# Group norm, 4-bit quantise and grouped 1x1 convolution: unrolled pipeline, ring of 12 images, coefficients for two images at a time

## The chip, the cores and the metric

The kernel runs on one core of a Trainium2 chip. The metric is device time in microseconds (us) of one execution, from the first to the last instruction and what the launch puts around them. It was measured three times before the change.

The core has five engines that run side by side, each in its own program order, and wait for one another on semaphores: TensorE (PE in the rows; PEld is its weight load), VectorE (DVE), ScalarE (ACT), GpSimd (POOL) and SyncE (SP), which here only issues DMAs.

## The reference, cut to what matters

`x` is (32, 512, 28, 28) in float32: 32 images, 512 channels, 784 pixels. Everything is one layer:

```python
v = _gn(x)                       # group norm: 32 groups of 16 channels, over 16*784 values, eps 1e-5
xg = v.reshape(B, 4, 128, H, W)[:, [1, 2, 3, 0]]
xa = round(clip((xg - lA) / (uA - lA), 0, 1) * 15) / 15
wq = (round(clip((weight - lW) / (uW - lW), 0, 1) * 15) / 15 - 0.5) * 2
y  = einsum('bgihw,goi->bgohw', xa, wq.reshape(4, 128, 128))
inv = gamma / sqrt(running_var + 1e-5)
y  = relu(y * inv + (beta - running_mean * inv))
out = x + (y + v)
```

## The kernel before, in words

**Tiling.** An image is `[128 partitions, 4 groups, 784]` float32, 1568 KB. Channel group g is a 128-channel slab, the contraction of one matmul. `images` is a ring of 8 such slots (`RING`). SP loads images in order, stores image n when DVE has added its four groups (semaphore `final`), and after each store issues the load that goes into the slot of the image before (L185 to L191). Most loops are hardware loops of 8 images with the first two and last six peeled off (`over_images`, L146).

**Per image, per engine, in program order:**

- DVE (`image` in the vector block): `cap` of groups 0 and 1 (min with 15, int16 to bf16, L409), statistics of the image two ahead (`bn_stats`, L398, six halves of 392 pixels: groups 0 to 2), `cap` of groups 2 and 3, a reciprocal of the standard deviation (L404), then `finish` for four groups (L420): `images = max(prod, floor) + images`, one operand from PSUM.
- ACT: the affine `images*y_scale + y_bias` of group 3 (L262); sum and squares of group 3 of the image two ahead (L223, L232); then `quantise` of the next image: four activations that write `levels` as int16 (L254), with `copy_mean` (L238) between the second and third, and `deviation` (L243, L244) behind them.
- POOL: `coefficients` of this image (L342 to L352, ten small instructions, a Newton step on `rough`), `sum_subsets` of the next (L321, L323), one `affine` of the image before (L360), `deviations` of the next (L330 to L335), which waits for `copy_mean`, and two `affine`s of this image.
- PE: `average_deviations` (L498) of the next image, four `multiply` of six matmuls each (L518: three bf16 parts of the weights times two halves), then `average_stats` (L492, L494).

Small instructions in one engine that read each other's result are fenced by a semaphore (`linked`, `chained`). The matmuls with `avg` sum over the 16 channels of a norm group. `prod` in PSUM has three sets of two banks; `PSUM_SET` gives set 0 to groups 0 and 3.

So the order of an image's coefficients is: statistics (DVE, ACT), sums (POOL), means (PE), copy (ACT), deviations (POOL), variance (PE), copy and root (ACT), reciprocal (DVE), coefficients (POOL), quantise (ACT), cap (DVE), matmuls (PE), and, with the affine of POOL, the addition (DVE).

Of the kernel before, what the change touches and what calls it, by code (L numbers as in the profile page):

```python
# [6 lines left out]
ACT = mybir.ActivationFunctionType  # L7
F32 = mybir.dt.float32
# [10 lines left out]
RING = 8  # L19
HEAD = 2  # L20
PARTS = 3
Y_ON_POOL = 3
STATS_ON_DVE = 3
PSUM_SET = (0, 1, 2, 0)
AHEAD = 2
# [3 lines left out]
def fused_norm_quantised_conv(nc, x, weight, limits, channel_params, out):  # L29
# [6 lines left out]
    SUBSETS = 4  # L36
    COUNT = HW // SUBSETS
    PAIRS = PER_NORM * SUBSETS
    assert C == G * P and B % RING == 0 and HALF <= nc.vector.BN_STATS_FMAX and HALF % 2 == 0

    TRIPS = B // RING
    x_v = x.rearrange("(t j) (g p) h w -> t j p g (h w)", p=P, j=RING)
    out_v = out.rearrange("(t j) (g p) h w -> t j p g (h w)", p=P, j=RING)

    with ExitStack() as ctx:
# [9 lines left out]

# [5 lines left out]
        stats = sb("stats", [P, 2, G, SUBSETS, 3], F32)  # L61
        x_sum = sb("x_sum", [P, 1], F32)
        unused = sb("unused", [P, HW], BF16)
        pair_sums = sb("pair_sums", [P, G, 2, 3], F32)
        stat_sums = sb("stat_sums", [P, 2, G, 3], F32)
        gmean = sb("gmean", [P, 2, G], F32)
        dev = sb("dev", [P, G, SUBSETS], F32)
        dev2 = sb("dev2", [P, G, SUBSETS], F32)
        dev2_pairs = sb("dev2_pairs", [P, G, 2], F32)
        dev2_sum = sb("dev2_sum", [P, G], F32)  # L70
        std = sb("std", [P, 2, G], F32)
        half_var = sb("half_var", [P, 2, G], F32)
        rough = sb("rough", [P, 2, G], F32)
        newt = sb("newt", [P, 3, G], F32)
        three_halves = sb("three_halves", [P, G], F32)
        rstd = sb("rstd", [P, G], F32)
        mean_q = sb("mean_q", [P, G], F32)
        mean_rstd = sb("mean_rstd", [P, G], F32)
        q_scale = sb("q_scale", [P, 2, G], F32)
        q_bias = sb("q_bias", [P, 2, G], F32)  # L80
        y_scale = sb("y_scale", [P, 2, G], F32)
        y_bias = sb("y_bias", [P, 2, G], F32)

# [8 lines left out]
        w_rng = sb("w_rng", [P, 3], F32)  # L92
        a_rng = sb("a_rng", [P, 4], F32)
        bn = sb("bn", [P, 8, G], F32)
        bias_bn = sb("bias_bn", [P, G], F32)
        floor = sb("floor", [P, G], F32)
        eps = sb("eps", [P, 3], F32)
        early = sb("early", [P, 1], F32)
        ident = sb("ident", [P, P], F32)
        avg = sb("avg", [P, P], F32)  # L100
        avg_n = sb("avg_n", [P, P], F32)

        prod = ps("prod", [P, 3, 2, 512], F32)
# [10 lines left out]
        weights_in = sem("weights_in")  # L114
        consts_done = sem("consts_done")
        eps_done = sem("eps_done")
        cols_done = sem("cols_done")
        bn_var_in = sem("bn_var_in")
        bn_std_done = sem("bn_std_done")
# [3 lines left out]
        params_ready = sem("params_ready")  # L123
        prep_step = sem("prep_step")
        consts_step = sem("consts_step")
        stats_done = sem("stats_done")
        moments_step = sem("moments_step")
        stats_summed = sem("stats_summed")
        mean_summed = sem("mean_summed")
        mean_ready = sem("mean_ready")  # L130
        dev_ready = sem("dev_ready")
        var_summed = sem("var_summed")
        std_ready = sem("std_ready")
        rough_ready = sem("rough_ready")
        coef_ready = sem("coef_ready")
        coef_step = sem("coef_step")
        quantised = sem("quantised")
        capped = sem("capped")
        y_ready = sem("y_ready")
        y_rest = sem("y_rest")  # L140
        multiplied = sem("multiplied")
        final = sem("final")

        def over_images(engine, image):  # L146


            for j in range(HEAD):
                image(0, j)  # L150
            with engine.Fori(0, TRIPS - 1) as t:
                for j in range(HEAD, HEAD + RING):
                    image(*later(t, 0, j))
            for j in range(HEAD, RING):
                image(TRIPS - 1, j)

        def output_group(g):

            return (g + G - 1) % G

        def later(t, j, by):
            return t + (j + by) // RING, (j + by) % RING

        def inside(t, j, by=0):

            return not isinstance(t, int) or 0 <= RING * t + j + by < B

        block = ctx.enter_context(nc.Block())

        @block.sync  # L170
        def _(sync):
            for g in (0, G - 1, 1, 2):
                sync.dma_start(images[:, 0, g], x_v[0, 0][:, g]).then_inc(first_loaded[g], DMA)
            sync.dma_start(w_raw[:], weight.rearrange("(g o) i -> o g i", o=P)).then_inc(weights_in, DMA)

            def load(t, j):
                if inside(t, j, -RING):
                    sync.wait_ge(stored[j], DMA * t)
                sync.dma_start(images[:, j], x_v[t, j]).then_inc(x_loaded[j], DMA)

            def store(t, j):
                sync.wait_ge(final, G * (RING * t + j) + G)
                sync.dma_start(out_v[t, j], images[:, j]).then_inc(stored[j], DMA)

            for j in range(1, RING):  # L185
                load(0, j)
            store(0, 0)
            with sync.Fori(0, TRIPS - 1) as t:
                for j in range(1, 1 + RING):
                    store(*later(t, 0, j))  # L190
                    load(*later(t, 0, j + RING - 1))  # L191
            for j in range(1, RING - 1):
                store(TRIPS - 1, j)
            for g in range(G):
                o = output_group(g)
                sync.wait_ge(final, G * (B - 1) + g + 1)
                sync.dma_start(out_v[TRIPS - 1, RING - 1][:, o],
                               images[:, RING - 1, o]).then_inc(stored[RING - 1], DMA)
            for j in range(RING):
                sync.wait_ge(stored[j], DMA * (TRIPS + (G - 1 if j == RING - 1 else 0)))  # L200

        @block.scalar
        def _(act):
            act.dma_start(rows[:], channel_params.rearrange("k (g p) -> (k g) p", p=P)).then_inc(rows_in, DMA)
            act.dma_start(bounds[:], limits.to_broadcast([P, 4])).then_inc(limits_in, DMA)
            act.wait_ge(eps_done, 1)

            nc.scalar.activation(early[:], eps[:, 0:1], ACT.Sqrt, bias=eps[:, 1:2])
            act.wait_ge(cols_done, 1)
            nc.scalar.activation(cols[:], cols_ps[:, 0:4 * G], ACT.Identity).then_inc(bn_var_in, 1)  # L210
            act.wait_ge(bn_var_in, 1)
            nc.scalar.activation(bn[:, 0], cols[:, 3], ACT.Sqrt, bias=eps[:, 1:2]).then_inc(bn_std_done, 1)

            last = G - 1

            def take_sum(t, j):

                n = RING * t + j
                if isinstance(t, int) and n == 0:
                    act.wait_ge(first_loaded[last], DMA)  # L220
                else:
                    act.wait_ge(x_loaded[j], DMA * t + (DMA if j else 0))
                nc.scalar.activation(unused[:], images[:, j, last], ACT.Identity,  # L223
                                     accum_out=x_sum[:]).then_inc(moments_step, 1)
                act.wait_ge(moments_step, 3 * n + 1)
                nc.scalar.activation(stats[:, j % 2, last, :, 1], x_sum[:].to_broadcast([P, SUBSETS]), ACT.Identity,
                                     scale=1.0 / HW).then_inc(moments_step, 1)

            def take_squares(t, j):

                act.wait_ge(moments_step, 3 * (RING * t + j) + 2)
                nc.scalar.activation(unused[:], images[:, j, last], ACT.Square, scale=-1.0,  # L232
                                     bias=stats[:, j % 2, last, 0, 1:2],
                                     accum_out=stats[:, j % 2, last, 0, 2:3]).then_inc(moments_step, 1)

            def copy_mean(t, j):
                act.wait_ge(mean_summed, RING * t + j + 1)
                nc.scalar.activation(gmean[:, j % 2], mean_ps[:, 0:G], ACT.Identity).then_inc(mean_ready, 1)  # L238

            def deviation(t, j):  # L240
                par = j % 2
                act.wait_ge(var_summed, RING * t + j + 1)
                nc.scalar.activation(half_var[:, par], var_ps[:, 0:G], ACT.Identity, bias=eps[:, 2:3], scale=0.5)  # L243
                nc.scalar.activation(std[:, par], var_ps[:, 0:G], ACT.Sqrt, bias=eps[:, 0:1]).then_inc(std_ready, 1)  # L244

            def quantise(t, j):
                n, par = RING * t + j, j % 2
                act.wait_ge(coef_ready, n + 1)
                if inside(t, j, -2):
                    act.wait_ge(capped, 2 * (n - 2) + 2)  # L250
                for g in range(G):
# [4 lines left out]
                if inside(t, j, 1):  # L256
                    deviation(*later(t, j, 1))
# [302 lines left out]
```

## Time and profile before

| what | us |
|---|---|
| runs of the kernel before | 298.91 (median), 296.23, 301.08 |
| span of the profiled execution, first to last instruction | 293.8 |
| median less this span | 5.1 |
| span over 32 images | 9.2 |
| DMA: 103.18 MB, mean 351 GB/s over the span | |

The profiled execution's own time is not given beside its span. The median of the runs less the span is used for what lies around it; by the lowest run it would be 2.4 us. Rows give microseconds from the span's start. An instruction's duration includes time in which it is issued and held, so neighbours overlap by some 0.1 us: the pitch from one start to the next is what a sequence costs.

### The profile page before, as it was taken

How to read it: one execution, taken by the hardware profiler on the slowest of the kernel's cores; microseconds unless marked ns; L12 is line 12 of the kernel's file. 1: busy time of each engine (PE TensorE's matmuls, PEld its weight loads, DVE VectorE, ACT ScalarE, POOL GpSimd, SP SyncE). 2: the span in 40 equal slices, each digit the busy share in tenths (PEclk: the TensorE clock that was granted, in tenths of full speed). 3: DMA queues.
4: the chain of work that ended last, by engine and by line, in shares of the span. 5: the costliest groups of instructions: out<-in, count | busy, mean ns of one | idle time of the engine just before them, and what ended most of it. 6: DMA issues, size and time to landing. Idle time of an engine off the chain costs nothing.

```text
span 293.8 us, 4567 instructions
## 1 busy us (share of the span) xinstructions
PE 192.5 (66%) x965; PEld 112.0 (38%) x965; DVE 265.6 (90%) x445; ACT 237.3 (81%) x420; POOL 214.4 (73%) x623
## 2 busy tenths in 40 slices
PE   0216757578686567575967768586766858686673
PEld 0104434344443334343543434344443434444331
DVE  1697999999999999999899998989999898989674
ACT  3347988888888999888888988888889888987760
POOL 2237887777887788877788787768878776887860
PEclk9999989977979979988695968869596886959688
DMA  5999989999999999999999999999999995555528
GB/s 184 402 410 410 409 333 365 373 400 392 386 403 389 407 404 389 386 389 386 404 351 406 380 380 374 364 406 333 412 361 386 382 365 207 219 219 217 203 115 342
DMA packets 34605, 103.18 MB, mean 351 GB/s; under 512 B 1296, under 2 KB 1824, under 8 KB 34592
## 3 DMA queue, kind: packets, MB, share of 16 engines
q1 hardware_dynamic: 34416, 103.03, 91.8%
q8 instruction: 4, 0.07, 0.1%
q10 hardware_dynamic: 176, 0.01, 0.1%
q14 instruction: 9, 0.07, 0.1%
HBM read 51.65 MB, written 51.38 MB: 351 GB/s over the span
## 4 chain that ended last, share of the span: by engine, by line
POOL 56%; issue 20%; PE 8%; DVE 6%; ACT 3%; POOLq 3%; DMA 2%; SPq 0%; DVEq 0%; ACTq 0%
POOL images L360 24%; PE prod L518 7%; POOL dev L333 4%; POOL dev_pairs L334 3%; POOLq L315 2%; ACT levels L254 2%; POOL dev L330 2%; POOL dev_sum L335 2%; DMA images<-in_x 2%; POOL pair_sums L321 2%; DVE images L420 2%; POOL newt L344 2%; POOL rstd L345 2%; POOL newt L343 2%; POOL q_scale L347 2%
## 5 line engine op out<-in xcount | busy, mean ns | idle before, releaser
L518 PE MATMUL prod<-codes,w_t 128*128 128x392 bf16 x768 | 168.4, 384 | 15.7 <-DVE images L420 13.4
L254 ACT ACTIVATE levels<-images,q_bias,q_scale 128x784 int16<-128x784 f32 x128 | 124.9, 1031 | 23.8 <-POOL q_bias L352 23.8
L420 DVE SCALAR_TENSOR_TENSOR images<-prod,floor,images 128x784 f32<-128x784 f32 x128 | 126.6, 1024 | 11.1 <-PE prod L518 10.1
L518 PEld LDWEIGHTS prod<-codes,w_t 128*128 128x128 bf16 x768 | 85.1, 115 | 90.5 <-issue 36.0
L360 POOL TENSOR_SCALAR images<-images,y_scale,y_bias 128x784 f32<-128x784 f32 x96 | 104.8, 1098 | 0.2 <-ACT levels L254 0.2
L398 DVE BATCH_NORM_STATS2 stats<-images 128x6 f32<-128x392 f32 x192 | 94.9, 546 | 7.3 <-DMA images<-in_x 7.2
L498 PE MATMUL var_ps<-dev_sum,avg 128*128 128x4 f32 x64 | 14.7, 301 | 61.5 <-POOL dev_sum L335 61.5
L409 DVE TENSOR_SCALAR codes<-levels 128x1568 bf16<-128x1568 int16 x64 | 45.1, 707 | 4.3 <-ACT levels L254 3.1
L498 PEld LDWEIGHTS var_ps<-dev_sum,avg 128*128 128x128 f32 x64 | 12.0, 234 | 64.2 <-POOL dev_sum L335 63.1
L262 ACT ACTIVATE images<-images,y_bias,y_scale 128x784 f32<-128x784 f32 x32 | 33.2, 1037 | 0.0
L232 ACT ACTIVATE unused<-images,stats 128x784 bf16<-128x784 f32 x32 | 30.3, 948 | 1.0
L330 POOL TENSOR_TENSOR dev<-stats,gmean 128x16 f32<-128x16 f32 x32 | 6.9, 216 | 30.2 <-ACT gmean L238 30.2
L223 ACT ACTIVATE unused<-images 128x784 bf16<-128x784 f32 x32 | 27.2, 850 | 2.2 <-DMA images<-in_x 2.2
L492 PE MATMUL mean_ps<-stat_sums,avg 128*128 128x4 f32 x64 | 9.6, 220 | 12.0 <-POOL stat_sums L323 12.0
L492 PEld LDWEIGHTS mean_ps<-stat_sums,avg 128*128 128x128 f32 x64 | 11.7, 198 | 14.5 <-POOL stat_sums L323 12.5
L321 POOL TENSOR_TENSOR pair_sums<-stats 128x24 f32<-128x24 f32 x32 | 7.7, 239 | 11.9 <-DVE stats L398 11.9
L238 ACT ACTIVATE gmean<-mean_ps 128x4 f32<-128x4 f32 x32 | 5.0, 158 | 11.5 <-PE mean_ps L492 11.5
L333 POOL TENSOR_TENSOR dev<-dev 128x16 f32<-128x16 f32 x32 | 12.2, 381 | 2.5
L243 ACT ACTIVATE half_var<-var_ps,eps 128x4 f32<-128x4 f32 x32 | 8.4, 263 | 5.6 <-PE var_ps L498 5.1
L494 PE MATMUL var_ps<-stat_sums,avg_n 128*128 128x4 f32 x64 | 12.1, 259 | 0.0
L494 PEld LDWEIGHTS var_ps<-stat_sums,avg_n 128*128 128x128 f32 x64 | 10.2, 201 | 0.0
L334 POOL TENSOR_TENSOR dev_pairs<-dev 128x8 f32<-128x8 f32 x32 | 7.8, 245 | 2.5
(66 smaller groups left out, 126.6 us busy)
## 6 DMA issues: line engine op xcount, KB each, us to landing
images<-in_x SPq DMA_DIRECT2D x31, 1568.0 KB, 10.9
out<-images SPq DMA_DIRECT2D x31, 1568.0 KB, 7.1
images<-in_x SPq DMA_DIRECT2D x4, 392.0 KB, 6.0
out<-images SPq DMA_DIRECT2D x4, 392.0 KB, 3.2
w_raw<-in_weight SPq DMA_DIRECT2D x1, 256.0 KB, 7.5
rows<-in_channel_params ACTq DMA_DIRECT2D x1, 8.0 KB, 2.9
bounds<-in_limits ACTq DMA_DIRECT2D x1, 2.0 KB, 5.9
```

The source lines that it names most:

```text
L223: nc.scalar.activation(unused[:], images[:, j, last], ACT.Identity, accum_out=x_sum[:]).then_inc(moments_step, 1)
L232: nc.scalar.activation(unused[:], images[:, j, last], ACT.Square, scale=-1.0, bias=stats[:, j % 2, last, 0, 1:2], accum_out=stats[:, j % 2 ...
L254: nc.scalar.activation(levels[:, par, g], images[:, j, g], ACT.Relu, bias=q_bias[:, par, g:g + 1], scale=q_scale[:, par, g:g + 1]).then_in ...
L262: done = nc.scalar.activation(images[:, j, g], images[:, j, g], ACT.Identity, bias=y_bias[:, par, g:g + 1], scale=y_scale[:, par, g:g + 1])
L333: linked(t, j, 3, nc.gpsimd.tensor_tensor(dev2[:], dev[:], dev[:], ALU.mult))
L360: nc.gpsimd.tensor_scalar(images[:, j, g], images[:, j, g], y_scale[:, par, g:g + 1], y_bias[:, par, g:g + 1], ALU.mult, ALU.add).then_inc ...
L398: done = nc.vector.bn_stats(two, images[:, j, g, h * HALF:(h + 1) * HALF])
L409: nc.vector.tensor_scalar(codes[:, j % 2, two], levels[:, j % 2, two], TOP, None, ALU.min).then_inc(capped, 1)
L420: nc.vector.scalar_tensor_tensor(out=two, in0=prod[:, PSUM_SET[g], :, 0:HALF], scalar=floor[:, o:o + 1], in1=two, op0=ALU.max, op1=ALU.add ...
L494: nc.tensor.matmul(var_ps[:, 0:G], avg_n[:], stat_sums[:, j % 2, :, 2], start=True, stop=False)
L498: nc.tensor.matmul(var_ps[:, 0:G], avg[:], dev2_sum[:], start=False, stop=True).then_inc(var_summed, 1)
L518: done = nc.tensor.matmul(prod[:, PSUM_SET[g], h, 0:HALF], w_t[:, part, output_group(g)], codes[:, j % 2, g, h * HALF:(h + 1) * HALF], sta ...
```

## The change

The loops are unrolled, and every engine is given a new order. In all of it n is an image, u = n // 2 a pair, and in each engine's loop the instructions for image n+1 stand at index n.

- `RING` 8 to 12, statistics five images ahead (`AHEAD` 5), 11 loads up front, then four stores, then two loads and two stores in turn.
- Statistics: DVE takes groups 0 and 1 (all three of 0 to 2 for the first four images), ACT groups 2 and 3. Two `tensor_reduce` per pair on DVE (`sum_stats`) take the place of `sum_subsets` on POOL.
- The chain mean, deviation, variance, coefficients runs once per pair. `rstd = var_eps ** -0.5` is one `tensor_tensor` with `ALU.pow` on POOL. The root on ACT, the reciprocal on DVE and the Newton step are gone.
- One `cap` per image, of 3136 elements, with max 0 and min 15.
- `quantise`: ACT does three groups of an even image and two of an odd one (image 0: two); POOL does the rest, as `tensor_scalar` to int16. All four affines are on POOL.
- PSUM sets in plain rotation; `average_means` stands behind the first `multiply` of image n+1, `average_deviations` behind the third.
- The preparation of the parameters and weights moves from DVE to POOL, for the most part.

The diff, cut to its core (three dots inside a line stand for arguments left out; lines with # name the engine):

```diff
-RING = 8
+RING = 12
-AHEAD = 2
+AHEAD = 5
+    def stats_on_dve(u):
+        return 3 if u < 2 else 2
+    def quant_on_act(n):
+        return 2 if n % 2 or n == 0 else 3
 # SP
+            for n in range(1, RING):
+                load(n)
+            for n in range(EARLY_STORES):
+                store(n)
+            for n in range(RING, B, 2):
+                load(n)
+                load(n + 1)
+                store(n - RING + EARLY_STORES)
+                store(n + 1 - RING + EARLY_STORES)
 # ACT
+            for n in range(-1, B):
+                u = (n + 3) // 2
+                chain = n % 2 == 1 and u < PAIRS
+                m = n + AHEAD
+                if m < B:
+                    take_sum(m, 2)
+                if chain:
+                    copy_mean(u)
+                if m < B:
+                    take_sum(m, 3)
+                    take_squares(m, 2)
+                    take_squares(m, 3)
+                if n + 2 < B:
+                    for g in range(quant_on_act(n + 2)):
+                        quantise(n + 2, g)
+                        if chain and g == 0:
+                            copy_var(u)
 # POOL
+            def deviations(u):
+                k, par = stats_on_dve(u), u % 2
+                pool.wait_ge(gmean_done, u + 1)
...
+                nc.gpsimd.tensor_tensor(dev[:, :, 0:k], ..., ALU.subtract)
+                nc.gpsimd.tensor_tensor(dev[:, :, k:G], ..., ALU.subtract).then_inc(dev_step, 1)
+                pool.wait_ge(dev_step, u + 1)
+                nc.gpsimd.tensor_tensor(dev2[:], dev[:], dev[:], ALU.mult).then_inc(dev_done, 1)
+            def coefficients(u):
+                par = u % 2
+                pool.wait_ge(var_copied, u + 1)
...
+                nc.gpsimd.tensor_tensor(rstd[:], var_eps[:], minus_half[:], ALU.pow).then_inc(coef_step, 1)
+                pool.wait_ge(coef_step, 2 * u + 1)
+                nc.gpsimd.tensor_tensor(mean_rstd[:], gmean[:, par], rstd[:], ALU.mult).then_inc(coef_step, 1)
+                nc.gpsimd.tensor_scalar(q_scale[:, par], rstd[:], a_rng[:, 2:3], None, ALU.mult)
+                nc.gpsimd.tensor_scalar(y_scale[:, par], rstd[:], 1.0, None, ALU.add)
+                pool.wait_ge(coef_step, 2 * u + 2)
+                nc.gpsimd.tensor_scalar(q_bias[:, par], mean_rstd[:], ..., ALU.mult, ALU.add)
+                nc.gpsimd.tensor_tensor(y_bias[:, par], ..., mean_rstd[:], ALU.subtract).then_inc(coef_done, 1)
+            def quantise(n):
+                u, j = n // 2, n % 2
+                pool.wait_ge(coef_done, u + 1)
+                if n >= 2:
+                    pool.wait_ge(capped, n - 1)
+                for g in range(quant_on_act(n), G):
+                    nc.gpsimd.tensor_scalar(levels[:, n % 2, g], images[:, n % RING, g], q_scale[...],
+                                            q_bias[...], ALU.mult, ALU.add).then_inc(q_pool, 1)
+            deviations(0)
+            coefficients(0)
+            quantise(0)
+            for n in range(-1, B - 1):
+                u = (n + 3) // 2
+                chain = n % 2 == 1 and u < PAIRS
+                affine(n + 1, 0)
+                if chain:
+                    deviations(u)
+                affine(n + 1, 1)
+                affine(n + 1, 2)
+                affine(n + 1, 3)
+                if n + 2 < B:
+                    quantise(n + 2)
+                if chain:
+                    coefficients(u)
 # DVE
+            def cap(n):
+                dve.wait_ge(q_act, q_act_until(n))
+                dve.wait_ge(q_pool, q_pool_until(n))
+                nc.vector.tensor_scalar(codes[:, n % 2], levels[:, n % 2], 0.0, TOP, ALU.max, ALU.min).then_inc(capped, 1)
+            for n in range(B):
+                m = n + AHEAD
+                finish(n, 0)
+                finish(n, 1)
+                if n + 1 < B:
+                    cap(n + 1)
+                finish(n, 2)
+                if m < B:
+                    half_stats(m, 0, 0)
+                finish(n, 3)
+                if m < B:
+                    half_stats(m, 0, 1)
+                    half_stats(m, 1, 0)
+                    half_stats(m, 1, 1)
+                    if m % 2 == 1:
+                        sum_stats(m // 2)
 # PE
+            def multiply(n, g):
+                k = G * n + g
+                pe.wait_ge(capped, n + 1)
+                if k >= SETS:
+                    pe.wait_ge(final, k - SETS + 1)
...
+            for n in range(-1, B - 1):
...
+                multiply(n + 1, 0)
+                if chain:
+                    average_means(u)
+                multiply(n + 1, 1)
+                multiply(n + 1, 2)
+                if chain:
+                    average_deviations(u)
+                multiply(n + 1, 3)
```

`affine(n, g)` and `finish(n, g)` work on output group (g + 3) % 4. `affine` waits for `coef_done` and, for groups that ACT quantises, for ACT's `quantise` of that group; it overwrites `images`. `cap` has no wait for POOL's affine.

## Rows read from the trace of the kernel before

**Rows 1.** Page: busy us by engine, GB/s in 40 slices; the cores: mean clock.

```profile
PE 192.5 (66%) x965; PEld 112.0 (38%) x965; DVE 265.6 (90%) x445; ACT 237.3 (81%) x420; POOL 214.4 (73%) x623
...
GB/s 184 402 410 410 409 333 365 373 400 392 386 403 389 407 404 389 386 389 386 404 351 406 380 380 374 364 406 333 412 361 386 382 365 207 219 219 217 203 115 342
...
core 0: 293.8 us, clock 0.856
```

**Rows 2.** Who waited for whom: us in total, times, longest us.

```profile
POOL dev L330 <- ACT gmean L238: 30.2, 32, 1.6
```

**Rows 3.** Timeline, POOL, one image: start us, us, instruction, count, idle before.

```profile
127.35 0.20 POOL L352 TENSOR_TENSOR q_bias<-a_rng,mean_q 128x4 f32<-128x4 f32 x1
...
129.79 0.21 POOL L330 TENSOR_TENSOR dev<-stats,gmean 128x16 f32<-128x16 f32 x1 [0.77 <-ACT gmean L238]
...
131.03 2.27 POOL L360 TENSOR_SCALAR images<-images,y_scale,y_bias 128x784 f32<-128x784 f32 x2
133.27 0.19 POOL L342 TENSOR_TENSOR newt<-rough 128x4 f32<-128x4 f32 x1
...
134.38 0.20 POOL L347 TENSOR_TENSOR q_scale<-rstd,a_rng 128x4 f32<-128x4 f32 x1
...
135.43 0.20 POOL L352 TENSOR_TENSOR q_bias<-a_rng,mean_q 128x4 f32<-128x4 f32 x1
```

**Rows 4.** Timeline, DVE, around the same image.

```profile
126.22 4.01 DVE L420 SCALAR_TENSOR_TENSOR images<-prod,floor,images 128x784 f32<-128x784 f32 x4
130.15 0.57 DVE L409 TENSOR_SCALAR codes<-levels 128x1568 bf16<-128x1568 int16 x1
...
131.60 0.84 DVE L409 TENSOR_SCALAR codes<-levels 128x1568 bf16<-128x1568 int16 x1
...
132.45 1.94 DVE L398 BATCH_NORM_STATS2 stats<-images 128x6 f32<-128x392 f32 x4
134.31 2.89 DVE L420 SCALAR_TENSOR_TENSOR images<-prod,floor,images 128x784 f32<-128x784 f32 x3
```

**Rows 5.** Timeline, ACT, the same image.

```profile
127.68 1.97 ACT L254 ACTIVATE levels<-images,q_bias,q_scale 128x784 int16<-128x784 f32 x2 [0.74 <-POOL q_bias L352]
129.56 0.15 ACT L238 ACTIVATE gmean<-mean_ps 128x4 f32<-128x4 f32 x1
...
132.77 0.85 ACT L223 ACTIVATE unused<-images 128x784 bf16<-128x784 f32 x1
...
133.98 0.95 ACT L232 ACTIVATE unused<-images,stats 128x784 bf16<-128x784 f32 x1
```

**Rows 6.** Timeline, start: sums on PE, the copy, the first additions.

```profile
23.25 0.59 PE L492 MATMUL mean_ps<-stat_sums,avg 128*128 128x4 f32 x2 [5.05 <-POOL stat_sums L323]
...
23.87 0.17 ACT L238 ACTIVATE gmean<-mean_ps 128x4 f32<-128x4 f32 x1 [4.05 <-PE mean_ps L492]
...
28.45 3.87 DVE L420 SCALAR_TENSOR_TENSOR images<-prod,floor,images 128x784 f32<-128x784 f32 x4
```

**Rows 7.** Page, part 6: KB, median us from issue to landing.

```profile
w_raw<-in_weight SPq DMA_DIRECT2D x1, 256.0 KB, 7.5
```

**Rows 8.** Timeline, last images: additions, affines, 24 matmuls.

```profile
278.36 1.03 DVE L420 SCALAR_TENSOR_TENSOR images<-prod,floor,images 128x784 f32<-128x784 f32 x1 [1.26 <-PE prod L518]
...
280.32 1.03 DVE L420 SCALAR_TENSOR_TENSOR images<-prod,floor,images 128x784 f32<-128x784 f32 x1 [0.93 <-PE prod L518]
...
281.38 2.95 POOL L360 TENSOR_SCALAR images<-images,y_scale,y_bias 128x784 f32<-128x784 f32 x3 [0.20 <-ACT levels L254]
...
284.80 4.15 PE L518 MATMUL prod<-codes,w_t 128*128 128x392 bf16 x24 [2.16 <-DVE codes L409]
286.08 4.02 DVE L420 SCALAR_TENSOR_TENSOR images<-prod,floor,images 128x784 f32<-128x784 f32 x4 [0.86 <-PE prod L518]
```

**Rows 9.** A stretch of 1 us; third figure from the end: TensorE clock.

```profile
279.00:280.00 1.00, 1.00 (x4) 0.45 (x3) 0.39 (x1) 0.00 (x0) 0.85 (x5) 0.50 0.49 186
```

**Rows 10.** Line L334, 128x8 elements on POOL: duration ns min/median/max.

```profile
L334 POOL TENSOR_TENSOR dev_pairs<-dev x32: 200/202/402, 12.5 to 275.1; 128x8 f32<-128x8 f32 x32
```

More of the change, by code:

```diff
@@ L206, in _ @@
             act.wait_ge(eps_done, 1)
[L208 to L227, printed above, removed]
@@ L240, in deviation @@
[L240 to L251, printed above, removed]
-                    if g == G // 2 and inside(t, j, 1):
-                        copy_mean(*later(t, j, 1))
-                    nc.scalar.activation(levels[:, par, g], images[:, j, g], ACT.Relu, bias=q_bias[:, par, g:g + 1],
-                                         scale=q_scale[:, par, g:g + 1]).then_inc(quantised, 1)
-                if inside(t, j, 1):
-                    deviation(*later(t, j, 1))
@@ new lines, in _ @@
+            for n in range(2):
+                take_sum(n, 3)
+                take_squares(n, 3)
+            copy_mean(0)
+            take_sum(2, 3)
+            take_squares(2, 3)
+            copy_var(0)
+            for g in range(quant_on_act(0)):
+                quantise(0, g)
+            take_sum(3, 3)
+            take_squares(3, 3)
+            for n in range(-1, B):
[15 more added lines that the diff above has]
+                            copy_var(u)
@@ L355, in affine @@
-            def affine(t, j, g):
-                par = j % 2
-                if not inside(t, j, 1):
-                    pool.wait_ge(quantised, G * (RING * t + j) + g + 1)
-                nc.gpsimd.tensor_scalar(images[:, j, g], images[:, j, g], y_scale[:, par, g:g + 1], y_bias[:, par, g:g + 1],
-                                        ALU.mult, ALU.add).then_inc(y_ready, 1)
-            def image(t, j):
-                coefficients(t, j)
-                if inside(t, j, 1):
-                    sum_subsets(*later(t, j, 1))
-                if inside(t, j, -1):
-                    affine(*later(t, j, -1), Y_ON_POOL - 1)
-                if inside(t, j, 1):
-                    deviations(*later(t, j, 1))
-                for g in range(Y_ON_POOL - 1):
-                    affine(t, j, g)
@@ L388, in chained @@
                 dve.wait_ge(prep_step, step[0])
-            def image_stats(t, j, g):
-                if isinstance(t, int) and (t, j) == (0, 0):
-                    dve.wait_ge(first_loaded[g], DMA)
-                elif g == 0:
-                    dve.wait_ge(x_loaded[j], DMA * t + (DMA if j else 0))
-                for h in range(2):
-                    two = stats[:, j % 2, g, 2 * h:2 * h + 2].rearrange("p s k -> p (s k)")
-                    done = nc.vector.bn_stats(two, images[:, j, g, h * HALF:(h + 1) * HALF])
-                if g == STATS_ON_DVE - 1:
-                    done.then_inc(stats_done, 1)
@@ new lines, in sum_stats @@
+            def sum_stats(u):
+                k, par = stats_on_dve(u), u % 2
+                dve.wait_ge(bn_done, halves_until(u))
+                if u >= 2:
+                    dve.wait_ge(var_done, u - 1)
+                for what in range(2):
+                    done = nc.vector.tensor_reduce(sums[:, par, what, :, 0:k], stats[:, par, :, 0:k, :, what + 1],
+                                                   AXIS.X, ALU.add)
+                done.then_inc(bn_summed, 1)
+            def cap(n):
+                dve.wait_ge(q_act, q_act_until(n))
+                dve.wait_ge(q_pool, q_pool_until(n))
+                nc.vector.tensor_scalar(codes[:, n % 2], levels[:, n % 2], 0.0, TOP, ALU.max, ALU.min).then_inc(capped, 1)
```

478 lines of the change are left out of this document (220 added, 258 removed).

## The prediction

> **What bounds the kernel now.** I began with the page's busy shares: DVE 90%, ACT 81%, POOL 73%, PE 66% [rows 1]. That alone says DVE. The waits say something else: POOL stands still once per image for the mean that ACT copies, 30.2 us over 32 images [rows 2]. So I walked one image in the timeline. POOL writes `q_bias` at 127.35 and does so again at 135.43: a period of 8.08 us [rows 3]. Between them lies a closed path: ACT starts `quantise` at 127.68, after its second group copies the mean at 129.56 [rows 5], POOL starts the deviations at 129.79, two affines at 131.03, the coefficients at 133.27, and ends `q_bias` at 135.63. Every step waits only for the one ahead of it. So the chain of coefficients, passed among POOL, ACT and PE, sets the pace, and DVE just keeps up.
>
> One row pair shows a second thing. POOL's two affines take 2.27 instead of 1.96 us, and the `cap` that DVE starts at 131.60, within the first of them, takes 0.84 where the one at 130.15 took 0.57 [rows 3, 4]. The cap ends at 132.44, about 0.42 after the first affine must have ended (131.03 + 0.98), and the second affine is late by 0.3. The two don't run together: cap waits for the POOL instruction in hand, and POOL's next one waits for cap. I count them as serial.
>
> The first additions start at 28.45 [rows 6] and the last end at 290.10, with 3.7 us to the end of the span [rows 8]: 8.4 us per image on average, above 8.08, because some images meet TensorE at its lower clock.
>
> **The change, part by part.** Prices: a POOL affine 0.98 (2.95/3), six matmuls at full clock 1.04 (4.15/4) and 1.96 at 1.2 GHz (278.36 to 280.32 between two additions that wait for matmuls, granted clock 0.50) [rows 8, 9]; an addition 0.98 (126.22 to 130.15, four), a half of `bn_stats` 0.465 (132.45 to 134.31, four) [rows 4]; two sums of small matmuls 0.62 from their start to the copy [rows 6]; the copy 0.15 and 0.08 to POOL's start [rows 3, 5].
>
> DVE gets lighter. Per pair: 8 additions 7.9, 8 halves of `bn_stats` 3.7, two caps of 3136 elements at about 0.84 + 0.14 (twice the 0.42, and 0.14 of issue from 0.57 less 0.42), two `tensor_reduce` at 0.2: 14.0 us, and near 15 with waits at the caps. The reciprocal goes. No row shows `tensor_reduce`; between 0.1 and 0.5 each it stays under the path below.
>
> ACT per pair: four sums at 1.0, four squares at 1.1, five `quantise` at 0.98, two copies: 13.7 us [rows 5]. Root and three small activations go.
>
> DMA moves the same bytes. The fullest slices reach 412 GB/s [rows 1]; 3.21 MB per image at 8.4 us are 382. A load is now issued when nine images before it is finished and used four images later: some 30 us of cover, against 8 us for two loads and 8 for two stores. Cost nothing; if cover went, only a few us of backlog.
>
> POOL is where the work lands: per pair 8 affines, 3 `quantise`, 3 instructions of deviations, 6 of coefficients. I lay out one pair, e = n+1 even, o = n+2 odd, from the end of POOL's `quantise` of e, in program order:
> - `affine(e, 0)` has nothing to wait for and starts at once: 0.98. The cap of e learns a hop later that its levels are there, so it waits for that affine, then 0.84: 1.82.
> - POOL's next is `deviations`, which waits for PE's means, which stand behind `multiply(e, 0)`, which waits for that cap. Hop 0.1, matmuls 1.04, means 0.62, copy and hop 0.23: 3.81. POOL is idle for 2.8 of it. Queued behind it are three affines and two quantises, and for those DVE's cap of o waits.
> - deviations, three instructions: 0.75 (four fenced ones took 131.03 less 129.79, 1.24 [rows 3]): 4.56. Three affines: 7.50. Two `quantise` of o at the price of an affine: 9.46.
> - The power, X. Cap of o takes its turn, 0.84. Five more small ones 1.0 (six took 1.25, 134.38 to 135.63 [rows 3]): 11.30 + X.
> - Four affines and one `quantise` of e+2: 16.20 + X, and the pair is closed.
>
> So a pair costs 16.20 + X + s, s being what the lower clock adds on `multiply(e, 0)` and the means.
>
> X: the nearest row is a POOL `tensor_tensor` on the same 8 elements per partition, 0.20 [rows 10]; the other end I take at 1.2, about the four fenced Newton instructions that it replaces (133.27 to 134.38). A power is surely more work per element than an add, but on eight elements; I take 0.5. POOL's `quantise` writes int16; no row shows it. At 0.98 as the affine; 0.8 to 1.3 would move a pair by -0.5 to +1.0.
>
> s: at 1.2 GHz the six matmuls cost 0.92 more and the means some 0.2: 1.1 in a pair that meets it. The mean clock of 0.856 [rows 1] means 29% of the time at the lower level. After the change PE is idle for about 1.6 us ahead of e but 3 ahead of o, so a fall should mostly hit o, whose matmuls have room: a quarter of the pairs, s = 0.25.
>
> [...]
>
> Pair: 16.20 + 0.50 + 0.25 = 16.95, or 8.48 per image, against 8.4 now. DVE's 15 and ACT's 13.7 fit inside, so what both save is idle time.
>
> Head: weights land 7.5 us after their issue [rows 7], about 10 us in. POOL, not DVE, now turns them to levels: four passes over 512 elements at 0.65 to 0.98 and four over 128, 5 us; deviations, PE and coefficients of pair 0 end near 19.5; two `quantise` 21.5; cap 22.5. DVE then does six halves and the reduces (25.7), means and copy bring POOL to 26.7, 0.75 + 2.94 + 1.96 to 32.3. In the layout this is 9.46, so the first pair begins at 22.9. Additions start near 27 to 28, as now: nothing won or lost.
>
> End: the last pair has no chain: affine and cap of 30 (1.82), three affines, two `quantise` (6.72), affine and cap of 31 (8.54), three affines (11.5), the last addition ends at 14.4; with the 3.7 of now [rows 8], 18.1.
>
> Sum: 22.9 + 15 × 16.95 + 18.1 = 295.3 us of span, against 293.8 now. The median of the runs is 5.1 above the span: 295.3 + 5.1 = 300.4 us.
>
> **The rivals.**
> *The chain is looser than I lay it (faster).* If cap of e gets its turn ahead of `affine(e, 0)`, POOL's idle time shrinks by 0.98 and the affine lies in it; with X at 0.2 a pair is 15.6, and 46.1 + 15 × 15.6 = 280.1 us. For it: the cap at 130.15 was hardly held up by small instructions. Against: POOL's affine needs no signal and cap does. The end of this line is DVE's 15 per pair: 271.
> *The power is slow (slower).* Place: the first instruction of `coefficients`, with cap of o and four affines behind it. From X = 0.85 the total passes 305; at 1.5 it is 17.95 per pair and 315.4 us. For it: elementwise power is in no row, and POOL's durations are the least known. Against: only eight elements.
> *TensorE is at 1.2 GHz on `multiply(e, 0)` in every pair (slower).* s = 1.1: 17.8 per pair, 313.1 us; from s = 0.6 the total passes 305. For it: PE's gaps are of the length of now's, 2 us and more. Against: the shorter gap is the one ahead of e.
>
> **How the numbers follow.** Forecast 300.4, chance 0.36; its own range, with X and s each moved by half, 294 to 306. Looser chain 0.32; slow power 0.18; low clock 0.14. The range takes in the first rival to near its own figure and the third: 281 to 313. What a measurement of this kernel can tell from no change is about 2%: 292.9 to 304.9. The looser chain gives faster 0.32; the two slow ones slower 0.32; the forecast the rest, within 2%, 0.36.
>
> **What would show it.** Right: POOL idle before the deviations for 2.5 to 3 us in each of 16 pairs, some 40 us in all, released by ACT's copy; DVE waiting for POOL's or ACT's levels ahead of the odd images' caps; caps near 1.8 us where they follow POOL's quantise and 0.98 elsewhere; pairs 17 us apart; busy shares of DVE and ACT down to about 80%. Wrong: DVE busy over 95% (then it paces, and the kernel is faster); a power of over 1 us; `quantise` on POOL far from 0.98; loads that statistics wait for in the middle of the run.

## The result, and the profile after

The changed kernel takes 312.8 us (median of four, 308.8 to 323.2), the kernel before 297.8 in the same comparison: ratio 1.041, 95% interval 1.034 to 1.048. It is slower. (The ratio is that of the executions that did not fall into a slower state of the core, 308.8 and 310.4 of the changed kernel; of all four the medians would give 1.051.) The profiled execution took 310.4 us, with a span of 308.7.

The page, parts 1 and 2, of the changed kernel:

```profile
PE 195.3 (63%) x997; PEld 111.1 (36%) x997; DVE 235.7 (76%) x339; ACT 190.7 (62%) x354; POOL 243.4 (79%) x349
...
GB/s 188 412 412 409 412 406 407 308 208 343 394 296 378 389 370 368 373 372 372 381 363 365 405 391 382 370 383 371 374 359 383 366 210 188 166 191 161 175 267 316
```

Against [rows 1], DVE lost 30 us of work and ACT 47, POOL gained 29, and no engine is busy for even 80% of the span. What fills the rest is in the waits (us in total, times, longest):

```profile
ACT gmean L234 <- PE mean_ps L492: 68.5, 16, 5.4
DVE codes L418 <- POOL levels L368: 45.2, 30, 3.9
POOL dev L329 <- ACT gmean L234: 44.5, 15, 5.3
```

POOL's wait for the mean, 30.2 us in [rows 2], is now 44.5 over half as many waits. The timeline of one pair, from the end of POOL's `quantise` of the even image (151.38) to the same point of the next pair (168.45); L359 is the affine, L329 the first deviation, L368 `quantise`, L343 the power:

```profile
151.38 0.99 POOL L359 TENSOR_SCALAR images<-images,y_scale,y_bias 128x784 f32<-128x784 f32 x1
155.07 0.21 POOL L329 TENSOR_TENSOR dev<-stats,gmean 128x16 f32<-128x16 f32 x1 [2.69 <-ACT gmean L234]
...
155.76 2.95 POOL L359 TENSOR_SCALAR images<-images,y_scale,y_bias 128x784 f32<-128x784 f32 x3
158.69 1.97 POOL L368 TENSOR_SCALAR levels<-images,q_scale,q_bias 128x784 int16<-128x784 f32 x2
160.62 1.67 POOL L343 TENSOR_TENSOR rstd<-var_eps,minus_half 128x8 f32<-128x8 f32 x1
162.37 0.20 POOL L345 TENSOR_TENSOR mean_rstd<-gmean,rstd 128x8 f32<-128x8 f32 x1
...
163.57 3.92 POOL L359 TENSOR_SCALAR images<-images,y_scale,y_bias 128x784 f32<-128x784 f32 x4
167.47 0.99 POOL L368 TENSOR_SCALAR levels<-images,q_scale,q_bias 128x784 int16<-128x784 f32 x1
168.45 0.99 POOL L359 TENSOR_SCALAR images<-images,y_scale,y_bias 128x784 f32<-128x784 f32 x1
```

The caps of that pair on DVE, and what PE and ACT do between the first cap and POOL's start at 155.07:

```profile
151.51 1.70 DVE L418 TENSOR_SCALAR codes<-levels 128x3136 bf16<-128x3136 int16 x1 [0.89 <-POOL levels L368]
...
160.76 0.98 DVE L418 TENSOR_SCALAR codes<-levels 128x3136 bf16<-128x3136 int16 x1 [1.92 <-POOL levels L368]
```

```profile
153.26 1.17 PE L510 MATMUL prod<-codes,w_t 128*128 128x392 bf16 x6 [2.28 <-DVE codes L418]
```

```profile
154.81 0.18 ACT L234 ACTIVATE gmean<-mean_ps 128x8 f32<-128x8 f32 x1 [4.51 <-PE mean_ps L492]
```

The closed path is there link by link: POOL's `quantise`, a cap held behind `affine(e, 0)`, six matmuls, means, copy, deviations. Its length is 17.07 us in most pairs: of the 14 periods between POOL's second and last deviations (33.39 and 274.49), 11 are 17.05 to 17.07, two 17.24 and 17.33, and one, which met TensorE at 1.2 GHz, 18.87.

### The profile page after: what moved, and what is told of

The parts are those of the page before. It is cut to its first block, busy times and chain, and to the rows that moved or that the text cites. A ratio compares the mean times of both kernels' runs of the same rounds, so it can differ in the third digit from the quotient of the medians.

```text
span 308.7 us, 3946 instructions
## 1 busy us (share of the span) xinstructions
PE 195.3 (63%) x997; PEld 111.1 (36%) x997; DVE 235.7 (76%) x339; ACT 190.7 (62%) x354; POOL 243.4 (79%) x349
## 4 chain that ended last, share of the span: by engine, by line
POOL 57%; issue 13%; PE 10%; DVE 10%; DMA 2%; ACT 2%; POOLq 1%; SPq 1%; DVEq 1%; ACTq 0%
POOL images L359 24%; POOL levels L368 15%; POOL rstd L343 9%; DVE codes L418 8%; PE prod L510 7%; DMA w_raw<-in_weight 2%; POOL q_bias L349 2%; PE mean_ps L492 1%; ACT levels L247 1%; POOL mean_rstd L345 1%; PE var_ps L500 1%; DVE images L426 1%; DVE stats L403 1%; POOL dev L329 1%; POOL y_bias L350 1%
## 5 line engine op out<-in xcount | busy, mean ns | idle before, releaser
L359 POOL TENSOR_SCALAR images<-images,y_scale,y_bias 128x784 f32<-128x784 f32 x128 | 127.3, 1007 | 0.2 <-issue 0.2
L247 ACT ACTIVATE levels<-images,q_bias,q_scale 128x784 int16<-128x784 f32 x79 | 78.2, 1029 | 11.0 <-POOL y_bias L350 11.0
L418 DVE TENSOR_SCALAR codes<-levels 128x3136 bf16<-128x3136 int16 x32 | 43.5, 1361 | 51.5 <-POOL levels L368 45.2
L403 DVE BATCH_NORM_STATS2 stats<-images 128x6 f32<-128x392 f32 x136 | 68.8, 552 | 3.6 <-DMA images<-in_x 3.6
L226 ACT ACTIVATE unused<-images,sums 128x784 bf16<-128x784 f32 x60 | 56.1, 936 | 0.1
L220 ACT ACTIVATE unused<-images 128x784 bf16<-128x784 f32 x60 | 50.7, 846 | 7.7 <-DMA images<-in_x 7.6
L368 POOL TENSOR_SCALAR levels<-images,q_scale,q_bias 128x784 int16<-128x784 f32 x49 | 48.4, 996 | 0.1
L329 POOL TENSOR_TENSOR dev<-stats,gmean 128x16 f32<-128x16 f32 (+1 forms) x16 | 3.5, 217 | 44.5 <-ACT gmean L234 44.5
L343 POOL TENSOR_TENSOR rstd<-var_eps,minus_half 128x8 f32<-128x8 f32 x16 | 27.0, 1685 | 2.8 <-ACT var_eps L240 2.8
L500 PEld LDWEIGHTS var_ps<-dev,avg 128*128 128x128 f32 x128 | 18.4, 211 | 1.2 <-issue 0.3
L500 PE MATMUL var_ps<-dev,avg 128*128 128x8 f32 x128 | 16.9, 259 | 0.0
L491 PEld LDWEIGHTS mean_ps<-sums,avg 128*128 128x128 f32 x32 | 6.4, 217 | 15.9 <-DVE sums L411 14.9
```

Source lines behind the costliest of these rows:

```text
L220: nc.scalar.activation(unused[:, g % 2], images[:, n % RING, g], ACT.Identity, scale=1.0 / HW, accum_out=sums[:, u % 2, 0, j, g:g + 1]).th ...
L226: nc.scalar.activation(unused[:, g % 2], images[:, n % RING, g], ACT.Square, scale=-1.0, bias=sums[:, u % 2, 0, j, g:g + 1], accum_out=sum ...
L247: nc.scalar.activation(levels[:, n % 2, g], images[:, n % RING, g], ACT.Relu, bias=q_bias[:, u % 2, j, g:g + 1], scale=q_scale[:, u % 2, j ...
L343: nc.gpsimd.tensor_tensor(rstd[:], var_eps[:], minus_half[:], ALU.pow).then_inc(coef_step, 1)
L359: nc.gpsimd.tensor_scalar(here, here, y_scale[:, u % 2, j, o:o + 1], y_bias[:, u % 2, j, o:o + 1], ALU.mult, ALU.add).then_inc(y_ready, 1)
L368: nc.gpsimd.tensor_scalar(levels[:, n % 2, g], images[:, n % RING, g], q_scale[:, u % 2, j, g:g + 1], q_bias[:, u % 2, j, g:g + 1], ALU.mu ...
```

## The experiments

Twelve kernels, each measured beside the kernel before. The changed kernel's profiled execution took 310.4 us; its pair of 17.07 us is what most of them are read against.

**1. The means ahead of the matmuls (means_first).** Only PE's order:

```diff
-                multiply(n + 1, 0)
                 if chain:
                     average_means(u)
+                multiply(n + 1, 0)
```

> Only PE's order is changed: average_means of the pair stands ahead of the first multiply of the even image, so POOL's deviations no longer wait for that image's cap and matmuls. Theory (a closed path through POOL's quantise, cap, six matmuls, means, copy, deviations sets the pair): POOL's idle time before the deviations (2.69 us per pair) goes, a pair falls from 17.07 to between 14.4 (POOL's own work) and 15.3 (DVE's work and holds), some 26 to 38 us less in all: 271 to 284 us where the changed kernel has 310. Rival (POOL or DVE is at its work limit, or the transfers are): within 3 us of the changed kernel, and the idle time turns up in front of another instruction.

Measured 287.2 us, ratio to before 0.977 (0.954 to 1.000). POOL no longer waits for the mean: it is busy for 90% of the span. Its deviations now meet the cap instead, and the next wait stands in ACT:

```profile
156.97 0.95 POOL L329 TENSOR_TENSOR dev<-stats,gmean 128x16 f32<-128x16 f32 x1
```

```profile
163.23 0.27 ACT L240 ACTIVATE var_eps<-var_ps,eps 128x8 f32<-128x8 f32 x1 [3.24 <-PE var_ps L500]
```

The pair alternates between 15.1 and 15.7, 15.4 on average. That is 3 us above the theory's range of 271 to 284, but 24 us below the changed kernel (profiled executions, 286.4 to 310.4); the rival is out.

**2. POOL's quantise earlier (quant_early).** POOL's order:

```diff
                 affine(n + 1, 1)
+                if n + 2 < B:
+                    quantise(n + 2)
                 affine(n + 1, 2)
                 affine(n + 1, 3)
-                if n + 2 < B:
-                    quantise(n + 2)
```

> Only POOL's order is changed: the quantise of the next image stands behind the second affine instead of the fourth. Theory: the cap of the even image starts while POOL still has three affines to do, so those fill the time in which it now waits for the means. Two affines, 1.96 us, move into the wait of 2.69: a pair of 15.1 us, about 282 us in all. Rival (DVE or the transfers set the pace): no more than 5 us less, with DVE busy as before but waiting elsewhere.

Measured 293.6 us (0.994, 0.987 to 1.001). Right in kind, short in size: a pair is 15.88 in most cases, not 15.1. DVE's cap of the odd image now waits for ACT (20.7 us in all), whose second `quantise` stands behind the variance. So it comes while POOL is at an affine, is held by it, and in turn holds the power, which takes 2.38 in place of 1.67 in most pairs. That 0.71 is nearly all that is missing:

```profile
102.40 1.68 DVE L418 TENSOR_SCALAR codes<-levels 128x3136 bf16<-128x3136 int16 x1 [0.98 <-ACT levels L247]
```

```profile
103.21 2.38 POOL L343 TENSOR_TENSOR rstd<-var_eps,minus_half 128x8 f32<-128x8 f32 x1
```

**3. No power (pow_to_sub).** The power of the pairs is left out; the coefficients, and with them the output, are other numbers.

```diff
-nc.gpsimd.tensor_tensor(rstd[:], var_eps[:], minus_half[:], ALU.pow)
+nc.gpsimd.tensor_tensor(rstd[:], var_eps[:], minus_half[:], ALU.subtract)
```

> In the coefficients of the pairs the power on POOL becomes a subtraction of the same shape, so the values of the output change and no work but the power is left out. The power takes 1.67 us, with its fence 1.75. If it is wholly on the path: 1.67 less 0.24, 1.43 per pair, 21 to 22 us less, 288 to 289 us. If the cap of the odd image, which now runs beside the power without holding anything up, then holds up the small instructions behind the subtraction for 0.84: 0.6 per pair, 9 us less, 301 us. Rival (POOL's coefficients are covered by ACT or DVE): no change.

Measured 296.9 us (1.007, 1.001 to 1.013), a pair of 16.32. What the power gave up, the cap of the odd image took back in part. The same two instructions, L345 on POOL and the cap on DVE:

```profile
169.37 0.90 POOL L345 TENSOR_TENSOR mean_rstd<-gmean,rstd 128x8 f32<-128x8 f32 x1
```

```profile
169.22 0.98 DVE L418 TENSOR_SCALAR codes<-levels 128x3136 bf16<-128x3136 int16 x1 [1.95 <-POOL levels L368]
```

With the power, L345 takes 0.20 and the cap runs to its end beside the power. So the second reading of the expectation holds (0.75 a pair measured, 0.6 expected; 296.9 us where it said 301). The spans differ by 13.8: 0.75 in each of 15 pairs, 0.7 in the head, and 1.8 in the one pair of the changed kernel that met 1.2 GHz. Without the power the kernel takes what the one before takes.

**4. The power twice (pow_twice).** Ahead of it, the same into an unused tile:

```diff
+                nc.gpsimd.tensor_tensor(spare[:], var_eps[:], minus_half[:], ALU.pow)
```

> The changed kernel with the power of the pairs computed twice, the first result unused. Theory (the power lies on the closed path): 1.6 to 1.7 us more in 15 of 16 pairs, 25 us more, 335 us. Rival (POOL's coefficients have cover): under 5 us more, 310 to 315.

Measured 355.7 us (349.3 to 359.9). The profiled execution took 353.3, 43 us more than the changed kernel's, where 25 were expected. A pair is 20.0 on average in place of 17.07, of which the power explains 1.64. The other part is on PE, in the six matmuls that the means wait behind, and in the clock of that stretch (third figure from the end; this kernel's lines stand two lower):

```profile
153.47 2.14 PE L512 MATMUL prod<-codes,w_t 128*128 128x392 bf16 x6 [3.40 <-DVE codes L420]
```

```profile
154.00:155.00 1.00, 1.00 (x4) 0.44 (x3) 1.00 (x3) 0.00 (x0) 0.00 (x0) 0.50 0.00 0
```

They ran at 1.2 GHz and took 2.14, where the changed kernel's took 1.17 at 2.4 GHz. POOL's wait for the mean went from 2.69 to 3.97 in most pairs. That is the prediction's third rival (1.1 per pair), which the changed kernel escapes in nearly all pairs and this one meets in most.

What takes the clock isn't settled by the length of the wait ahead of the matmuls (3.40 here, 2.28 in the changed kernel). The granted clock had fallen before that wait, with the last matmuls of the image before:

```profile
149.00:150.00 1.00, 1.00 (x6) 0.41 (x5) 0.75 (x1) 1.00 (x2) 1.00 (x2) 0.98 0.89 336
150.00:151.00 1.00, 0.08 (x1) 0.00 (x0) 0.00 (x0) 0.50 (x2) 1.00 (x2) 0.50 1.03 414
```

In another pair of pow_twice a wait of 3.23 was followed by 1.17, and in the one long pair of the changed kernel a wait of 1.78 by 2.03:

```profile
213.47 1.17 PE L512 MATMUL prod<-codes,w_t 128*128 128x392 bf16 x6 [3.23 <-DVE codes L420]
```

```profile
66.62 2.03 PE L510 MATMUL prod<-codes,w_t 128*128 128x392 bf16 x6 [1.78 <-DVE codes L418]
```

The clock also fell in the changed kernel's odd image, whose matmuls nothing on the path waits for: 0.50 from 163 to 165 in the pair above. The Trainium skill, TensorE: Matmul & The Clock Gate, section "HAM oscillation — how this bites in real kernels", tells of a kernel that waits for DMA between its bursts of matmuls and loses the clock in every such wait. These runs agree in part: of the changed kernel's two waits in the pair above (2.28 and 2.60), only the second was followed by a fall.

**5. The affine out of the cap's way (affine_behind).** POOL's order:

```diff
-                affine(n + 1, 0)
                 if chain:
                     deviations(u)
+                affine(n + 1, 0)
```

> Only POOL's order is changed: the first affine of an even image stands behind the deviations instead of ahead of them, so the cap of that image finds POOL idle. Theory: the cap takes 0.98 instead of 1.70 and the deviations start about 0.8 us sooner, but one more affine (0.98) follows them: a pair is the same or longer by 0.1 to 0.2 us, 309 to 313 us in all. Rival (the cap's hold behind POOL's affine is itself what costs): 0.8 less per pair, 12 us less, 298 us.

Measured 312.9 us (312.6 to 313.3), a pair of 17.36. As the theory has it, the caps take 0.98 each, and the affine that filled the wait is now behind it; the pair is 0.3 longer, where 0.1 to 0.2 was expected. The hold of a cap costs nothing where an affine gets done meanwhile.

**6. The ring (ring8).** 

```diff
-RING = 12
+RING = 8
-EARLY_STORES = 4
+EARLY_STORES = 2
```

> The changed kernel with a ring of 8 images and two early stores instead of 12 and 4. Theory (compute is the bound and the loads have cover): the same time within 5 us, 308 to 315, with a few waits for loads. Rival (the longer ring carries the changed kernel, which would be slower still without it): 8 us more or above.

Measured 314.7 us (308.4 to 318.2), within the scatter of the changed kernel. ACT waited for images ten times, 14.4 us in all, where the changed kernel has 7.6. The pairs are 17.11 but for a few; four late ones are 18.4 to 19.0, and in these POOL waits 3.97 for the mean, behind matmuls at 1.2 GHz as in pow_twice. Apart from those pairs the two kernels agree, so the longer ring neither cost nor gained here; whether it has a part in the four isn't shown.

**7. The whole chain first (chain_first).** On top of means_first:

```diff
                 multiply(n + 1, 0)
+                if chain:
+                    average_deviations(u)
                 multiply(n + 1, 1)
                 multiply(n + 1, 2)
-                if chain:
-                    average_deviations(u)
```

> PE's order alone: average_means stands ahead of the first multiply of the even image and average_deviations right behind it (in means_first it is behind the third). In means_first ACT waits 3.2 us for the variance in the middle of the odd image's quantise, and the cap of that image 1.0 us for it. Theory: that wait was the next piece of the closed path; with it gone POOL's own work is left, 11 operations of 0.98 and 4.1 of small ones with two holds by caps of about 0.8, 15.0 us per pair against 15.4 in means_first: 278 to 282 us. Rival (transfers or DVE's work set the pace in means_first already): the same time as means_first, 285 to 288.

Measured 285.3 us (0.959, 0.952 to 0.965). Pairs of 15.06 and 15.73 by turns, POOL busy for 91% of the span. The gain over means_first is 2 us. The theory's 278 to 282 was missed by 3 and the rival's 285 to 288 met, so two more runs (9 and 10) had to tell POOL's work from the transfers.

**8. Both (chain_first_early).** chain_first with quant_early's order.

> chain_first, and POOL's quantise behind the second affine as in quant_early. Theory: nothing waits on the path any more, so the two changes don't add: POOL's work of 15 us a pair remains, 276 to 282 us. If the gains did add (the two shorten different waits) it would be below 270, which DVE's work of 14.3 per pair and transfers at 410 GB/s (7.8 us per image) exclude.

Measured 285.2 us (0.958, 0.952 to 0.964), 3 above the expected range: no gain on 7. The two shorten the same wait.

**9. chain_first with no power (chain_no_pow).** The edit of 3 on top of 7; the power is left out as there.

> chain_first with the power of the pairs as a subtraction; the output changes, and of the work only the power is left out. It asks what bounds chain_first (15.4 us per pair, POOL busy throughout, transfers at 405 GB/s). Theory (POOL's own work): 1.43 per pair less, less a new hold by the odd image's cap of up to 0.8: 0.6 to 1.4 per pair, 9 to 20 us, 265 to 276 us. Rival (transfers): 6.42 MB per pair at 410 GB/s are 15.7 us, so loads or DVE hold it, the time stays within 4 us of 285 and statistics wait for loads.

Measured 271.0 us (0.908, 0.899 to 0.918), inside the theory's range.

**10. chain_first with ACT taking all of the even image (chain_act4).**

```diff
-        return 2 if n % 2 or n == 0 else 3
+        return 2 if n % 2 or n == 0 else 4
```

> chain_first with all four groups of an even image quantised by ACT, so POOL has one operation of 0.98 less per pair and ACT one of 0.97 more (ACT's work 14.3 per pair). Theory (POOL's own work bounds chain_first): 0.5 to 0.98 per pair less, 7 to 14 us less, 271 to 278 us. Rival (transfers, or ACT at once as long as POOL): within 3 us of 285.

Measured 270.7 us (0.908, 0.898 to 0.917). With 9 and 10 both 14 us below chain_first, POOL's own work was its bound; the rival is out. chain_act4 computes all that the reference has, and is 9% faster than the kernel before. Its page:

```profile
PE 187.1 (69%) x997; PEld 109.4 (41%) x997; DVE 225.0 (83%) x339; ACT 205.1 (76%) x369; POOL 239.2 (89%) x334
...
GB/s 158 407 414 410 410 410 405 405 402 342 365 370 403 408 403 409 398 408 408 400 405 403 408 406 399 411 401 409 399 407 408 399 412 400 400 401 353 288 190 300
```

Transfers run at about 405 GB/s almost to the end, 15.9 us for the 6.42 MB of a pair, while its pairs are 14.3: it lives off the ring's lead. Late in both kernels that lead gives out: ACT's statistics wait for an image once in chain_act4 (1.88 us, at 220) and three times in chain_no_pow (6.3 us, from 188 on). That two kernels with different cuts both end at 271 fits a limit by the transfers, but wasn't tried by itself.

**11. The weights on DVE (chain_head).** In chain_first, the eight weight instructions move from POOL to DVE, between the statistics of images 0 and 1, and PE's transposes ahead of the first means.

> chain_first with the weights' eight instructions on DVE, between the statistics of images 0 and 1, and PE's transposes ahead of the first means. On POOL they took 8.8 us, 10.2 to 19.0, and the deviations of pair 0 waited for them, as did PE's transposes, 2 us of PE. Theory: the first coefficients come 1.5 to 2.5 us sooner and the whole is that much shorter, 283 us. Rival (the late statistics of image 1 set the head, which lands 13.9 us in): under 1 us.

Measured 285.1 us against 285.3: nothing. The first deviations start at 18.80 in place of 18.96. The rival holds: image 1's statistics, from 13.9 (14.2 in chain_head), lead to ACT's copy of the mean at 18.2 (18.5).

**12. The same one line on the changed kernel (act4_alone).**

> The changed kernel with all four groups of an even image quantised by ACT and PE's order as the change has it. On the closed path POOL's quantise of the even image (0.98) lies between its four affines and the cap; ACT, idle for 4.5 us a pair ahead of the copy, has the fourth group done by the time those affines end. Theory (closed path): 0.9 to 1.0 per pair less, 14 us less than the changed kernel, 294 to 298 us, and POOL's wait for the mean stays at 2.7 us a pair. Rival (the wait absorbs what POOL is spared, since work was never POOL's bound): within 4 us of the changed kernel, 307 to 313, and the wait grows to 3.6.

Measured 286.5 us (0.955, 0.946 to 0.963): 1.7 per pair less, almost twice what the theory gave, and POOL's wait fell instead of staying. POOL, DVE at the start of the even image, and POOL's deviations:

```profile
153.91 1.77 POOL L359 TENSOR_SCALAR images<-images,y_scale,y_bias 128x784 f32<-128x784 f32 x1 [0.16 <-ACT levels L247]
156.68 0.21 POOL L329 TENSOR_TENSOR dev<-stats,gmean 128x16 f32<-128x16 f32 x1 [1.00 <-ACT gmean L234]
```

```profile
153.85 0.97 DVE L418 TENSOR_SCALAR codes<-levels 128x3136 bf16<-128x3136 int16 x1
```

The affine now waits 0.16 for ACT's last `quantise`, and the cap comes straight behind DVE's additions, 0.06 ahead of it. So the cap goes through in 0.97 and the affine, 1.77 long, is held. That is the prediction's first rival, the cap ahead of the affine, come about in this kernel: of the 1.72 gained per pair 0.98 is the spared `quantise`, and some 0.7 is the cap's turn, where the rival gave 0.98.

## Why the prediction came out as it did

It said 300.4 us and "within 2%" as likeliest; the result, 312.8, is 4% slower, outside that class and 0.2 us inside the upper end of the range (313). The path was right, its terms were not all, and that the miss stayed this small is partly luck: errors of opposite sign met, in the pair and around the span.

| term | predicted | measured in the changed kernel |
|---|---|---|
| end of `quantise(e)` to deviations | 3.81 | 3.69 |
| deviations, three affines, two `quantise` | 5.65 | 5.55 |
| the power, X | 0.50 | 1.75 (1.67 and the fence) |
| cap of o, taking its turn | 0.84 | 0 |
| five small instructions | 1.00 | 1.20 |
| four affines, one `quantise` | 4.90 | 4.88 |
| pair without clock | 16.70 | 17.07 |

**The power** is the step that failed. I set it between 0.2 and 1.2 and took 0.5; 1.67 is above the upper end, which was no bound at all: nothing tied the Newton instructions' time to that of one power. The rival had named 1.5 and 315 us. pow_to_sub shows the counterfactual: 296.9 us, where the prediction's own sum with X = 0.2 gives 295.9. So close an agreement is luck too: its pair is 16.32 where that sum has 16.65, and its head and end are longer.

**The odd cap** was the error the other way. "Cap of o takes its turn, 0.84": it runs beside the power in full. The prediction treated every POOL instruction as holding the cap, from one affine's row. This hid two thirds of the power's excess of 1.25.

**The head** was 6.6 us short. The prediction's 22.9 for the start of the first pair is counted back from the end of POOL's `quantise` of image 1, which it put at 32.3; measured it is 38.94. Of this, 5.6 us had gone by when the first `quantise` ended, at 27.1 in place of 21.5. Read from the timeline, image 1's statistics began only at 13.91, the copies of mean and variance came at 18.23 and 21.71, and the first power took its 1.67; how the 5.6 divides among them wasn't tried. The weights on POOL, which took 8.8 us for my 5, have next to no part in it (chain_head). The first deviations and the first power:

```profile
18.96 0.23 POOL L329 TENSOR_TENSOR dev<-stats,gmean 128x24 f32<-128x24 f32 x1
...
22.05 1.67 POOL L343 TENSOR_TENSOR rstd<-var_eps,minus_half 128x8 f32<-128x8 f32 x1 [2.38 <-ACT var_eps L240]
```

**The end** was 2.7 short: the last addition ended at 301.89, 14.0 after `quantise(30)` (14.4 as laid out), but 6.8 us of stores followed, not 3.7. The last whole image went out only just ahead of the four last groups:

```profile
291.58 6.94 SPq L182 DMA_DIRECT2D out<-images  x2
299.09 4.23 SPq L198 DMA_DIRECT2D out<-images  x4
```

Sum: head 6.6, the pairs from there on 4.1 (17.22 on average instead of 16.95), end 2.7 are the 13.4 us between 295.3 and 308.7. Against it stood 5.1 us around the span, taken from a median and another execution's span; in the profiled one it is 1.7, which hid 3.4 of the 13.4.

**The clock** cost 0.15 per pair (17.22 less 17.07), where 0.25 was given, and 1.8 of these 2.1 us fell in one pair. Transfers, DVE's and ACT's work had the cover that the prediction gave them: statistics waited for images only in the first 18 us.

Of its five signs of being right four came: POOL idle ahead of the deviations, 44.5 us for "some 40"; DVE waiting for levels ahead of the odd caps; caps of 1.70 and 0.98; pairs 17 us apart. The busy shares of DVE and ACT fell further than the 80% given, to 76 and 62%. One sign of being wrong came as well, a power of over 1 us.

## What to carry to other kernels

Walk one period of a pipeline from a fixed point back to itself, through every engine's program order. Where a small reduction stands in a queue behind a large step that it does not need, the large step is on the path: one moved line was worth 7 to 8% here. Work that leaves the busiest engine is worth nothing while such a path is longer than that engine's work. And an operation that no row shows has no upper bound from rows of other operations; try it by itself, or let the range say so.

## What the runs showed of the hardware

- A power on POOL takes 1.67 us for 8 elements per partition and 1.05 for 4 (in the preparation), where a subtraction or multiplication of two tiles takes 0.20 for either.
- DVE's cap waits for a POOL affine in hand (1.70 for 0.98) and holds a POOL instruction that comes after it (0.90 for 0.20), but ran in full beside POOL's power when the power had started first. A power that came behind a cap was held (2.38 for 1.67 in quant_early).
- Which of cap and affine goes first isn't told by the recorded starts alone. In the changed kernel the affine starts 0.13 us ahead and the cap is held, in act4_alone the cap starts 0.06 ahead and the affine is held. But in three pairs of chain_act4 the affine's record starts 0.13 to 0.15 ahead, and it is the affine that is held:

```profile
218.44 1.82 POOL L359 TENSOR_SCALAR images<-images,y_scale,y_bias 128x784 f32<-128x784 f32 x1 [0.16 <-ACT levels L247]
```

```profile
218.59 0.97 DVE L418 TENSOR_SCALAR codes<-levels 128x3136 bf16<-128x3136 int16 x1
```

- `tensor_scalar` on POOL with multiply and add costs 0.62 for 512 elements and 0.98 for 784, also with int16 out; subtract and multiply cost 2.08, max and min 1.92, a lone multiply to int16 1.50 for 512. On DVE (chain_head) the four instructions below took 0.53, 0.43, 0.43 and 0.43, in their order. What makes them differ on POOL wasn't tried:

```profile
L315 POOL TENSOR_SCALAR w_rest<-w_raw,bounds,w_rng 128x512 f32<-128x512 f32 x1 | 2.1, 2083 | 3.3 <-DMA w_raw<-in_weight 3.3
L316 POOL TENSOR_SCALAR w_rest<-w_rest 128x512 f32<-128x512 f32 x1 | 1.9, 1924 | 0.1
L317 POOL TENSOR_SCALAR w_lev<-w_rest 128x512 int16<-128x512 f32 x1 | 1.5, 1497 | 0.1
...
L318 POOL TENSOR_SCALAR w_rest<-w_lev 128x512 f32<-128x512 int16 x1 | 0.6, 618 | 0.1
```
